# First attention of a five-stage kernel: batch 0 projected from half of the norm, q and k split by halves over several heads, and the pieces of the dequantization put in the last batch

## The reference, cut to what matters

```python
x = x + _L0_attn_ref(_layernorm(x, axis=-1), w_qkv, q_norm_w, k_norm_w, w_o)
# _L0_attn_ref: 16 heads of 16, window 128
qkv = hidden_states @ w_qkv.T
q, k, v = jnp.split(qkv, 3, axis=-1)
q = _rope(heads(_rms_norm(q, q_norm_w)))
k = _rope(heads(_rms_norm(k, k_norm_w)))
mask = (q_idx >= k_idx) & (q_idx - k_idx <= WINDOW - 1)
scores = jnp.where(mask, jnp.einsum('bhqd,bhkd->bhqk', q, k) * scale, -jnp.inf)
out = jnp.einsum('bhqk,bhkd->bhqd', softmax(scores), v)
return out @ w_o.T
# stage 2: w = (q.astype(float32) - 7.5) * repeat(scale, 64, axis=1)
```

## Time and profile before

| | us |
|---|---|
| median of 3 runs | 1214.65 (1208.97, 1214.65, 1230.64) |
| the profiled execution, its own time | 1207.77 |
| its span, first to last instruction | 1205.9 |
| PE busy in the span | 1077.4 (89%) |
| DVE, ACT, POOL busy | 826.9, 622.5, 593.7 |
| first attention, to the first row maximum | 49.7 |
| its four batches, head 0 to head 0 | 45.2, 38.7, 36.1, 22.3 |

### The profile page before, as it was taken

The page is one execution under the profiler, slowest core; times in us unless marked ns, Lnnn a source line. Parts: engine busy times, 40 slices in busy tenths (PEclk is TensorE's granted clock), DMA queues, the critical chain, the costliest instruction groups (busy, mean ns, idle before and its releaser), DMA issues. The chain is left out here.

```text
span 1205.9 us, 22149 instructions
## 1 busy us (share of the span) xinstructions
PE 1077.4 (89%) x6760; PEld 926.5 (77%) x6760; DVE 826.9 (69%) x1987; ACT 622.5 (52%) x1881; POOL 593.7 (49%) x621
## 2 busy tenths in 40 slices
PE   2689896797699848999999999999988999999998
PEld 1578785487455427999899989999977888888887
DVE  7555674644888876888787878888875555555555
ACT  1444562222799725666576567666653333343332
POOL 4344200353477554665465556554533555455553
PEclk9877998599799968999999999999997999999999
DMA  8000001000223120002002000000001111111111
GB/s 241 1 1 1 1 1 22 1 1 1 107 88 100 66 90 1 2 6 76 3 2 79 3 3 1 2 2 1 1 9 44 43 52 41 51 49 42 52 39 48
DMA packets 43826, 41.41 MB, mean 34 GB/s; under 512 B 6016, under 2 KB 39840, under 8 KB 43728
## 3 DMA queue, kind: packets, MB, share of 16 engines
q1 hardware_dynamic: 42000, 39.02, 10.7%
q10 hardware_dynamic: 1728, 1.18, 0.3%
HBM read 39.08 MB, written 1.11 MB: 33 GB/s over the span
## 5 line engine op out<-in xcount | busy, mean ns | idle before, releaser
L1900 POOL TENSOR_TENSOR hid_l<-hid,hid_h 128x512 fp32r<-128x512 f32 x66 | 85.6, 1296 | 132.5 <-ACT hid_h L1869 132.5
L1526 POOL TENSOR_TENSOR qr<-r_part_a,r_part_b 128x512 f32<-128x512 f32 x64 | 82.5, 1289 | 117.8 <-DVE r_part_b L1560 117.6
L1540 POOL TENSOR_TENSOR prob<-prob,rden 128x128 f32<-128x128 f32 (+1 forms) x256 | 123.9, 508 | 23.2 <-DVE rden L1611 22.7
L1950 DVE TENSOR_TENSOR hid<-psum,silu 128x512 f32<-128x512 f32 x66 | 45.7, 692 | 130.5 <-ACT silu L1867 130.5
L1486 ACT ACTIVATE prob<-psum,neg_max 128x128 f32<-128x128 f32 (+1 forms) x256 | 105.4, 419 | 41.6 <-DVE neg_max L1600 34.6
L1942 DVE SCALAR_TENSOR_TENSOR x<-psum,weight,x 128x256 f32<-128x256 f32 x264 | 108.9, 476 | 0.0
L73 PE MATMUL psum<-xt_h,gu_l 128*128 128x512 f32 x264 | 106.1, 402 | 2.4 <-POOL gu_l L1885 2.4
L75 PE MATMUL psum<-xt_h,gu_h 128*128 128x512 f32 x264 | 105.0, 398 | 0.0
L74 PE MATMUL psum<-xt_l,gu_h 128*128 128x512 f32 x264 | 104.5, 396 | 0.0
L1867 ACT ACTIVATE silu<-psum 128x512 f32<-128x512 f32 x66 | 39.5, 598 | 118.9 <-PE psum L75 118.9
L1073 POOL TENSOR_TENSOR drive<-u,b_all 128x1024 f32<-128x1024 f32 x32 | 75.7, 2367 | 41.3 <-DVE h L1189 20.5
(11 more groups left out here) (269 smaller groups left out, 3617.9 us busy)
## 6 DMA issues: line engine op xcount, KB each, us to landing
b_all<-scan_b_rows SPq DMA_DIRECT2D x16, 512.0 KB, 3.6
early<-in_L_ffn_Wq_dram SPq DMA_DIRECT2D x4, 1024.0 KB, 6.0
early<-in_L_ffn_Wo_dram SPq DMA_DIRECT2D x4, 1024.0 KB, 8.4
raw<-in_L_ffn_Wg_dram SPq DMA_DIRECT2D x32, 128.0 KB, 2.2
raw<-in_L_ffn_Wu_dram SPq DMA_DIRECT2D x32, 128.0 KB, 2.3
raw<-in_L_ffn_Wd_dram SPq DMA_DIRECT2D x32, 128.0 KB, 2.2
x<-_attn_hidden_states_dram SPq DMA_DIRECT2D x8, 128.0 KB, 4.5
early<-in_L_ffn_w_up_q_dram SPq DMA_DIRECT2D x1, 1024.0 KB, 7.2
```

Of the source, the lines that this page charges most:

```text
L1526: pool.tensor_tensor(qr[:, i, :], part_a[:, slot, :], part_b[:, slot, :], ALU.add).then_inc(roped, 1)
L1540: ins = pool.tensor_tensor(at, at, rden[:, s % 4, i:i + 1].to_broadcast([P, (i + 1) * P]), ALU.mult)
L1900: pool.tensor_tensor(hid_l[:, j, cols], hid[:, c, :], f(hid_h[:, j, cols]), ALU.subtract)\
```

## The change

The norm's functions are cut in steps that can be called for one half. TensorE projects tiles 0 and 1 when half 0 is through and GpSimd's low weights are made; the second half of the norm is normalised, transposed and split between the steps of these tiles. The clearing of `k_t` goes to the front, one half of it on GpSimd and the other on VectorE, of the rows and places that are read as zero alone. The projection weights come in two DMAs behind the identity on ScalarE's queue, `wo` moves to the end of SP's own loads. GpSimd's low weights wait for the four tiles of half 0 to be normalised. In the batches the two halves of a split are steps of their own (slots 3 and 4 for t0, 8 and 9 for t1), `qkv` of t1 moves from slot 3 to slot 5, t1's transposes are ordered q, k, q, k in slots 9 to 12, and the first scores of a quad wait for the first tile of q and k only. All eight pieces of the dequantization stand in the last batch.

```diff
         def schedule():
             yield "qkv", 0
+            yield "normalise_rest",
             yield "qkv", 1
-            yield "split", 0
-            for i in range(4):
+            yield "turn_rest",
+            for n in range(2):
+                yield "split", 0, n
+            yield "low_rest",
+            for i in ORDER[0]:
                 yield "turn_qk", 0, i
...
                     if b + 1 < B:
                         if slot == 0:
                             yield "qkv", t0
-                        if slot == 3:
+                        if slot in (3, 4):
+                            yield "split", t0, slot - 3
+                        if slot == 5:
                             yield "qkv", t1
-                            yield "split", t0
                         if 4 <= slot < 8:
-                            yield "turn_qk", t0, slot - 4
-                        if slot == 7:
-                            yield "split", t1
-                        if 9 <= slot < 12:
-                            yield "turn_qk", t1, slot - 9
-                        if slot == 11:
-                            yield "turn_qk", t1, 3
+                            yield "turn_qk", t0, ORDER[0][slot - 4]
+                        if slot in (8, 9):
+                            yield "split", t1, slot - 8
+                        if 9 <= slot < 13:
+                            yield "turn_qk", t1, ORDER[1][slot - 9]
                     yield "dequantize", h
...
+                norm.scalar(act, (0,))
+                act.wait_ge(zeroed, 2)
+                def turn_rest():
+                    norm.scalar(act, (1,))
+                    act.wait_ge(loaded_o, 16)
+                    act.activation(wo_h[:], wo_raw[:], ACT.Copy).then_inc(w_hi, 1)
...
+                pool.memset(f(k_t[0:P // 2, :, :, 1, :]), 0.0).then_inc(zeroed, 1)
                 pool.memset(v[:], 1.0).then_inc(zeroed, 1)
-                pool.wait_ge(w_hi, 1)
-                pool.tensor_tensor(w_l[:], w_raw[:], f(w_h[:]), ALU.subtract).then_inc(w_ready, 1)
                 pool.wait_ge(pool_own, 1)
-                norm.gpsimd(pool)
-                pool.memset(f(k_t[:]), 0.0).then_inc(zeroed, 1)
+                norm.gpsimd(pool, (0,))
+                pool.wait_ge(norm.normed, TH)
+                for k in range(KD):
+                    pool.wait_ge(w_hi, k + 1)
+                    pool.tensor_tensor(w_l[:, k, :], w_raw[:, k, :], f(w_h[:, k, :]), ALU.subtract).then_inc(w_ready, 1)
+                norm.gpsimd(pool, (1,))
...
-                    if 12 <= h < 12 + 2 * ffn.PIECES:
-                        ffn.dequantize(pool, h - 12)
+                    b, slot = h // NH0, h % NH0
+                    if b == B - 1 and slot % 2 == 0:
+                        ffn.dequantize(pool, slot // 2)
...
-                norm.vector(dve, core.x, [(loaded_x[h], 16 * TH) for h in range(2)])
+                norm.begin(dve)
+                own.add(dve.memset(f(k_t[P // 2:P, :, :, 0, :]), 0.0))
+                norm.stats(dve, core.x, 0, arrived)
+                norm.normalise(dve, core.x, 0)
+                norm.stats(dve, core.x, 1, arrived)
+                norm.low(dve, 0)
...
-                pe.wait_ge(loaded_c, 16 * 7)
-                norm.tensor(pe)
-                pe.wait_ge(w_ready, 1)
-                norm.ready(pe, 1)
+                pe.wait_ge(loaded_i, 16)
+                norm.tensor(pe, (0,))
+                pe.wait_ge(w_ready, KD)
+                norm.ready(pe, 0)
```

More of the change, by code:

```diff
@@ L99, in __init__, with begin @@
         self.y = sb(f"{tag}_y", [P, NT, D], F32)
[L101 to L113, removed]
-            own.settle()
+    def begin(self, dve):
+        self.count = Count(dve, self.own)
+        self.scale = self.rs if self.twice is None else self.rs2
@@ L115, in vector, with normalise @@
+    def normalise(self, dve, x, h):
+        own, ts = self.count, slice(h * TH, (h + 1) * TH)
+        if self.twice is not None:
+            dve.wait_ge(self.rstd_ready, self.vars_before + 2 + h + 1)
+            own.add(dve.tensor_tensor(self.rs2[:, ts], self.rs2[:, ts], self.rs[:, ts], ALU.mult))
+            own.settle()
+        else:
+            dve.wait_ge(self.rstd_ready, self.vars_before + h + 1)
+        for t in range(h * TH, (h + 1) * TH):
             if self.rms:
-                own.add(dve.tensor_tensor(self.ve2[:, ts], self.mv[:, ts, 0], self.mv[:, ts, 0], ALU.mult))
@@ L135, in vector @@
[L135 to L148, removed]
@@ L149, in vector @@
-        self.low(dve)
-        if self.z is not None:
-            for t in range(NT):
-                own.add(dve.tensor_scalar(self.z[:, t, :], x[:, t, :], self.mv[:, t, 0:1], self.rs[:, t:t + 1],
-                                          ALU.subtract, ALU.mult))
-        own.settle()
-    def low(self, dve):
-        for n, (half, k) in enumerate((h, k) for h in range(2) for k in range(KD)):
-            bank = self.c.psum[:, 2 * half + k, :]
+                ins = dve.tensor_scalar(self.y[:, t, :], x[:, t, :], self.scale[:, t:t + 1], None, ALU.mult)
+            else:
+                ins = dve.tensor_scalar(self.y[:, t, :], x[:, t, :], self.mv[:, t, 0:1], self.scale[:, t:t + 1],
+                                        ALU.subtract, ALU.mult)
@@ L175, in gpsimd, with tensor @@
             pool.tensor_tensor(to[:, ts], src[:, ts], self.c.neg_half[:, 0:TH], ALU.pow).then_inc(self.rstd_ready, 1)
-    def tensor(self, pe, y=None):
-        for half in range(2):
+    def tensor(self, pe, halves=(0, 1)):
+        for half in halves:
             for t in range(half * TH, half * TH + TH):
```

174 lines of the change are left out of this document (111 added, 63 removed).

## The result

The changed kernel takes 1233.55 us (median of five runs, 1230.02 to 1243.98) beside 1211.06 for the kernel before (1208.97 to 1230.64): 1.0192 times as long, with a 95% interval of 1.0152 to 1.0231, or 22.5 us. The forecast was 1215, with 1187 to 1240 as its range; the time lies in the range and 18.6 us above the forecast, which stood level with the 1214.65 then known for the kernel before. The profiled run is the slowest of the five, 1243.98 (span 1242.2), where that of before is 1207.77, under the five.

What follows compares the result with a forecast made beforehand. Nothing is full at the start and TensorE sets the pace in the batches. Start and full-clock batches save 14.1 us, 1207.8 to 1193.7; half clock adds 20.7, giving 1214, written as 1215, range 1187 to 1240.

Steps and rivals of the forecast that it cites:

- The start: Before the batches: earlier first projection (15.4) and first row maximum (near 40.3); gain 9.4 us, bounds 7.5 and 11.3.
- The new wait in slot 5: Three batches: TensorE's transposes after t1's projection wait about 3.0 us for VectorE's rotary parts, between 1.7 and 3.6.
- waits of slots 9 and 10: t1's split halves stand behind exponentials in slots 8 and 9: waits of 0.8 and 1.4 us, bounds 0 and 3 together.
- The price of the order at full clock: Per batch: old waits cost 3.6 and new ones 6.3 us, so 2.7 slower, 38.8 for batch 1 or 2.
- The dequantization: Eight pieces leave batch 0 and start behind t1's `qr` in batch 2, ending early in batch 3; 1.0 us lost, batch 39.8.
- The clock: Slot 5 wait brings half clock in each of three batches: 11.5 us in batch 0, 4.6 each in 1 and 2, 20.7 total.
- full-clock batches of the forecast: Batches 0 to 2 without any clock fall: 36.7, 38.8 and 39.8 us, 4.7 less than before.
- The clock stays down: Rival: projecting out at slot 8 fails to restore the clock in batches 1 and 2; 1238 to 1244 us, chance 0.17.
- No lasting fall: Rival: the slot 5 wait is there, but the clock stays or returns at once; 1194 to 1201 us, chance 0.25.
- no new wait: Rival: slot 5 wait is 1.7 and old 0.87 and 1.03 go; batches 33, 35, 36; 1183 us, chance 0.13.

Runs made afterwards that it cites:

- e7: e1 plus fourteen matmuls nobody reads in TensorE's slot 9 wait of batch 0, ahead of head 8's values; 1188.7 us, 0.980 of the kernel before.
- e9: Kernel before, plus only fourteen matmuls nobody reads in TensorE's 3.62 us wait in slot 9 of batch 0; 1199.9 us, 0.991 of the kernel before.
- e12: e11 plus one more unread matmul ahead of the transposes of heads 0 to 3 of every batch; 1207.7 us, 0.994 of the kernel before.
- e4: Changed kernel with the dequantization put back at heads 12 to 19; 1233.1 us, 1.016 of the kernel before.
- e5: Changed kernel plus one unread 512-column matmul ahead of the transposes of every head, 64 in all; 1204.5 us, 0.997 of the kernel before.
- e6: Changed kernel plus two unread matmuls ahead of the transposes of heads 1 to 4 of batch 0 alone; 1232.4 us, 1.011 of the kernel before.
- e8: e2 plus nine unread matmuls in TensorE's slot 9 wait of batch 0 and of batch 2; 1188.2 us, 0.980 of the kernel before.
- e10: e8 plus twelve unread matmuls ahead of the first transposes of tile 0 and of tile 1 at the start; 1189.2 us, 0.980 of the kernel before.
- e11: Changed kernel plus unread matmuls only where its transposes wait in the batches, none in slots 0 to 3; 1215.1 us, 1.000 of the kernel before.
- e1: Changed kernel's start only; batch order, wait of the scores and dequantization place from the kernel before; 1201.5 us, 0.991 of the kernel before.
- e2: e1 with the dequantization in the last batch, as in the changed kernel; 1222.0 us, 1.008 of the kernel before.
- e3: Changed kernel with t1's projection put back from slot 5 to slot 3; 1224.7 us, 1.006 of the kernel before.

## Why the prediction was right or wrong

**The start**: forecast 9.4, bounds 7.5 and 11.3; 7.7 in the profile, 10.0 between the heads 0 of e7 and e9, 11.1 between their medians. The steps to the first projection held (16.31 for 15.4, since the statistics ended 0.87 later than before), and the clearing cost nothing, 3.47 us and over at 5.13. Tile 0's transposes begin at 29.87 for 28.3. The transposes of the second half of the norm stand behind the projection of tile 1, so they start at 25.74, when VectorE's tiles have been there since 24.0. That is the clock again, but for 0.4 to 0.6 by which the first projection begins earlier in other runs: in the profiled run this projection takes 4.0 us at half clock (21.73 to 25.74), in e7 and e12, which have the same start, 2.2 at full clock; there the transposes of the norm start at 23.35 and 23.53 and those of tile 0 at 27.41 and 27.59, 0.9 and 0.7 ahead of the forecast. The forecast counted no half clock at the start.

**The new wait in slot 5**: forecast 3.0, not below 1.7 nor above 3.6; 3.04 in e4, 2.56 and 2.58 in e5, 2.41 in e6, where the projection ran at full clock. The chain through VectorE's order was right (0.6, 1.5 and 2.2 make 4.3 on TensorE's side, not 4.2, which changes nothing). In the changed kernel itself it is 1.04, 1.11 and 1.04. The text took full clock for the stretch in which it let the clock fall. The waits of slots 9 and 10 (0.8 and 1.4 forecast) are 0.81 and 1.19 in batch 1.

**The price of the order at full clock**: forecast 2.7 a batch. Batch 2 of e12 is 40.34 where e8, with the same dequantization and the old order, has 37.41: 2.9, of which four fills are at most 0.9 (3.19 / 14 = 0.23 each), so between 2.0 and 2.9. In batch 1 of e5, at full clock too, it is 4.0 (40.06 for 36.05), of which sixteen fills are at most 3.6, so 0.4 or more. The forecast is not contradicted; no run has the new order at full clock without fills. Its own sum is loose: the old waits it names are 2.9 together and the new ones 6.1, which is 3.2 more, and the 3.6 and 6.3 are not worked out.

**The dequantization**: forecast in batch 2, from behind t1's `qr`, 1.0 more there and 1.33 less in batch 0. GpSimd is busy 28.56 us in batch 2, and the eight pieces run from 168.75 to 192.6, so they end in batch 2 and not, as forecast, in batch 3, which the half clock has put off. At full clock it costs 1.36 there (37.41 in e8, 36.05 in e7) and saves 1.33 in batch 0 (34.82 in e10, 36.15 in e7). Both were measured in the old order, and there the direct price was right. The Trainium skill, "SBUF — State Buffer", section "Who interferes with whom", would have let a half of the split wait for a whole instruction of GpSimd, 1 to 2 us more. In the changed kernel the two halves of batch 2 show both cases, GpSimd first, then VectorE's halves and TensorE's wait behind the second:

```profile
177.53 1.49 POOL L781 TENSOR_SCALAR early<-early 128x512 f32<-128x512 int32 x1
182.21 1.27 POOL L783 TENSOR_TENSOR early<-early 128x512 f32<-128x512 f32 x1
```

```profile
178.74 0.68 DVE L585 TENSOR_TENSOR stack<-qr,stack 128x512 fp32r<-128x512 f32 x1
182.22 1.80 DVE L585 TENSOR_TENSOR stack<-qr,stack 128x512 fp32r<-128x512 f32 x1 [1.43 <-ACT stack L459]
```

```profile
184.17 0.63 PE L676 MATMUL psum<-ident,stack 128*128 128x128 f32 x4 [2.14 <-DVE stack L585]
```

The second half begins 0.01 behind a TENSOR_TENSOR of 1.27 and takes 1.12 longer than the first: there the trace agrees with the page. The first half meets the end of a TENSOR_SCALAR and loses nothing, so one half pays and not both, and the smaller sum was the better one. The tiles beside the clearing, which the forecast named as agreeing, are another case: they have one tile as input, and GpSimd's instruction there only writes.

**The clock is the step that failed, in trigger and size.** That the time is in the range all the same is owed to the width of the range, not to this step. The forecast said that a new wait of 3 us brings half clock in each batch, from slot 5 or 6, and 11.5 + 4.6 + 4.6 = 20.7 us. Against the full-clock batches of the forecast (36.7, 38.8, 39.8, 22.3) the measured ones are 12.7, 10.7, 10.2 and 11.9 longer, 45.5 in all; these 24.8 more, 1.7 less at the start and 3.2 in the rest make the 30 between 1214 and 1244 (by the medians the miss is 18.6). Batch 0 has nearly its forecast, by another way. Batches 1 and 2 fall twice, in slot 4 and in slots 9 and 10 or on the way to the next batch, and projecting out once does not cover both. Batch 3, priced at nothing, runs at 0.61. The trigger is wrong in three ways: the fall at 53.17 needs no wait above 0.63; the waits of 2.41 in e6, of 2.58 in e5 and of 2.14 in the changed kernel itself (184.17, full clock until 193.12) are followed by none in the next 8 us; and with the waits filled (e11) the clock falls all the same. What the runs show is that the clock can fall in light work (transposes, products of 17 columns) with short waits in it, that a long wait in it often has a fall in it or close behind (3.62, 3.61, 3.04, 2.56, 2.28 and 2.21 had one; 2.58, 2.41 and 2.14 had none), and that a piece of dense work in time can prevent it (e5, e7, e8, e9); full clock came back behind a projection more than once, not always. The change took the projection out of slot 3, so that the fall there, 3.4 us in e1, e2 and e3, lasted 47.8. That the spread splits matter, by longer light stretches with more short waits, is not shown: together with what goes with them they cost 2.7 or nothing from e2 to e3.

The Trainium skill, "TensorE: Matmul & The Clock Gate", section "A second HAM failure mode: psum-queue depth-cycling", states that in a kernel of bf16 matmuls of 512 columns short idle times between groups of matmuls make the clock swing between its two levels. The rows from 50.17 to 53.36 agree in so far as the only wait ahead of the fall is 0.63; the 47.8 us of half clock behind it, with TensorE busy for 46.8, are more than a swing. By that rule, which I did not weigh, the falls would have had to be counted from the light slots on.

**The rivals.** "The clock stays down", 1238 to 1244 for the profiled run, gives the profiled run's time, but half of its mechanism is not in this kernel: projecting out did bring the clock back, at 179.47 and 220.43. In e3, e6 and e11 it failed to in batch 3, as that rival said (39.9, 40.6 and 39.8 us for 22.3). "No lasting fall" and "no new wait" fell. The forecast's frame, a gain at the start spent in the batches by half clock, was right; its amount was not.

**Open**: what decides in a given run whether a light stretch tips the clock. Twelve runs of e3 lie between 1206.3 and 1229.4, those of e11 as far apart (1199.7 to 1224.8), and only one run of each kernel has a trace.

## What to carry to other kernels

A kernel whose pace TensorE sets has a second resource, its clock, and moving a dense piece of work away from light ones can cost more than any wait that the move removes: look at the work between two dense pieces, not for the longest wait alone. A price found at full clock says nothing of what it triggers, so a change is best tried beside a version that fills TensorE's waits with matmuls that nobody reads: 14 of them, 3.2 us in a wait of 3.7, gave 12 us here, and took the 20 us away that the late dequantization had seemed to cost.

## What was not expected of the hardware

- The clock fell with TensorE waiting no longer than 0.63 us at a time (53.17), and stayed at 0.50 for 47.8 us in which TensorE was busy for 46.8.
- A dense projection at half clock did not bring it back in slot 5 of batch 0 (57.34 to 61.5), while behind others it came back: in slot 5 of batch 1 (110.73 to 114.8, back at 114.61) and in slot 0 of batches 1 and 2 (95.86 to 100.1, back at 100.96; from 145.40, back at 148.75).
- 64 matmuls of 512 columns that nobody reads made a kernel 29 us faster (e5), and the twelve runs of another (e11) lay up to 25 us apart, the longer ones at the lower mean clock (0.943 to 0.916).
